# Group sums by shuffles on VectorE, a scaled expert added by DMA, and ScalarE's steps in another order

## The reference

```
h   = x + silu(bn(sum over e of sigmoid(mean(gn(x)) @ w_route.T + b_route)[e] * conv3x3(gn(x), w_experts[e])))
out = h + conv3x3(gn(h), sign(W))
```

## Time and profile before

| | |
|---|---|
| Time, median of 3 runs | 272.57 us (272.32 to 272.82) |
| Profiled execution: its own time | 272.72 us |
| Its span, first to last instruction | 270.6 us |
| Busy PE / DVE / ACT / POOL | 263.6 / 254.6 / 213.0 / 45.5 us |
| Granted TensorE clock | 1.000 in the mean |
| One stage (from `group_stats` to `group_stats`) | 15.50 us |

### The profile page before, as it was taken

One profiled execution on the slowest core, in us unless ns is written; L12 is line 12 of the kernel. 1 busy time (PEld: TensorE's weight loads), 2 busy tenths in 40 slices (PEclk: granted clock), 3 DMA queues, 4 the chain that ended last, 5 costly groups with the idle time before them and its releaser, 6 DMA issues.

```text
span 270.6 us, 4214 instructions
## 1 busy us (share of the span) xinstructions
PE 263.6 (97%) x1339; PEld 182.5 (67%) x1339; DVE 254.6 (94%) x461; ACT 213.0 (79%) x469; POOL 45.5 (17%) x61
## 2 busy tenths in 40 slices
PE   8899999999999999999999999999999999999993
PEld 7554857668595766759486776849576675948573
DVE  5799999999999999999999999999999999995984
ACT  2798898898979787997979798897979796736860
POOL 2012120313121120312112021212112021210120
PEclk9999999999999999999999999999999999999999
DMA  6998945552617355452726456261735536272407
GB/s 202 417 388 279 325 150 156 78 155 32 127 78 131 104 79 155 58 134 54 145 80 97 136 79 159 27 128 80 125 108 80 157 47 128 70 136 87 78 2 155
DMA packets 10245, 35.20 MB, mean 130 GB/s; under 512 B 1264, under 2 KB 1904, under 8 KB 10224
## 3 DMA queue, kind: packets, MB, share of 16 engines
q0 software_dynamic: 4176, 15.21, 33.1%
q1 hardware_dynamic: 5616, 19.34, 19.1%
q10 hardware_dynamic: 432, 0.39, 0.4%
HBM read 11.34 MB, written 16.25 MB: 102 GB/s over the span
## 4 chain that ended last, share of the span: by engine, by line
PE 95%; DVE 2%; issue 1%; POOL 0%; ACT 0%; DVEq 0%; POOLq 0%
PE pc L599 43%; PE pa L562 14%; PE pb L562 14%; PE pe_ L562 14%; PE pd L552 6%; PE pd L488 2%; PE ps L531 1%; PE ps L535 1%; DVE U L1178 0%; PE pa L636 0%; PE pb L636 0%; DVE X L1404 0%; PE pc L521 0%; POOL rstd L446 0%; DVE sums L1386 0%
## 5 line engine op out<-in xcount | busy, mean ns | idle before, releaser
L1188 DVE SCALAR_TENSOR_TENSOR U<-we,route,U 128x1152 f32<-128x1152 f32 x45 | 63.7, 1415 | 0.5
L599 PE MATMUL pc<-lo,ws 128*128 128x496 f16 (+3 forms) x270 | 62.0, 375 | 0.0
L599 PE MATMUL pc<-hi,ws 128*128 128x496 f16 (+3 forms) x270 | 59.8, 375 | 0.1
L599 PEld LDWEIGHTS pc<-hi,ws 128*128 128x128 f16 x270 | 26.4, 98 | 29.6 <-issue 0.5
L599 PEld LDWEIGHTS pc<-lo,ws 128*128 128x128 f16 x270 | 27.7, 106 | 26.3
L446 POOL TENSOR_TENSOR rstd<-ve,nhalf 128x2 f32<-128x2 f32 (+1 forms) x19 | 17.5, 923 | 141.4 <-ACT ve L856 120.1
L562 PE MATMUL pa<-V,UM 128*128 128x256 f32 (+1 forms) x180 | 40.7, 375 | 0.0
L562 PE MATMUL pb<-V,UM 128*128 128x256 f32 (+1 forms) x180 | 40.6, 375 | 0.0
L562 PE MATMUL pe_<-V,U 128*128 128x256 f32 (+1 forms) x180 | 40.5, 375 | 0.0
L562 PEld LDWEIGHTS pb<-V,UM 128*128 128x128 f32 x180 | 34.1, 190 | 5.5 <-issue 0.7
L562 PEld LDWEIGHTS pe_<-V,U 128*128 128x128 f32 x180 | 34.2, 190 | 3.9
(11 more groups left out here) (168 smaller groups left out, 400.9 us busy)
## 6 DMA issues: line engine op xcount, KB each, us to landing
X<-x SPq DMA_DIRECT2D x15, 512.0 KB, 5.6
out<-X SPq DMA_DIRECT2D x15, 512.0 KB, 2.6
out<-ev POOLq DMA_DIRECT2D x15, 512.0 KB, 5.5
X<-y POOLq DMA_DIRECT2D x14, 512.0 KB, 4.5
we<-w_experts SPq DMA_DIRECT2D x2, 768.0 KB, 8.2
ws_raw<-w_sign SPq DMA_DIRECT2D x1, 576.0 KB, 10.4
we<-w_experts SPq DMA_DIRECT2D x1, 512.0 KB, 6.2
out<-X SPq DMA_DIRECT2D x1, 384.0 KB, 3.0
```

Of the source, the lines that this page charges most:

```text
L599: mm = mm_(rows[:, r0 - first // W:r1 - first // W, c0:c1], ws[:, tap * C:(tap + 1) * C], plane((hi, lo)[part], i)[:, r0 + ky - 1:r1 + ky ...
L1188: v.scalar_tensor_tensor(out=nine(U[i % RING]), in0=expert(e), scalar=route[:, i, e:e + 1], in1=nine(U[i % RING]), op0=ALU.mult, op1=ALU.a ...
```

## The change

Three things.

1. The group values of slots 4 to 17 (stages 2 to 15; "slots 2 on" counts from the stage) no longer come from PE. DVE makes them: `group_sums(c)` exchanges neighbouring partitions by a shuffle and adds, then partitions two apart and adds, which leaves the sum over four channels in `gsum` in SBUF. In stages 2 to 14 it stands behind `inner_rows`, in stage 15 in front of `sign_points`. The readers on ACT take `gsum` and a scale of 1/4 in place of PSUM, and ACT gets one more instruction, `middle_mean`. Slots 1 to 3 and the last one stay on PE.
2. For images 3 to 15 DVE's `mix(i, 1)` is gone. ACT writes expert 1 times its route into a new tile `scaled` (`scale_second`, behind `mix`), and POOL issues a DMA that adds `scaled` (128x1152 float32) to `U`. DVE's `mix(i, 2)` waits for it.
3. In ACT's stage `bias` and `split_hi` stand ahead of `deviation`, `centring` and `pads`.

```diff
+SCALED_FROM = 3
...
+        def first_mix(i):
+            return 2 if i >= SCALED_FROM else 1
...
+        def by_shuffles(c):
+            return LAG < c < CHAINS - 1
+        def group_means(c, a, b):
+            return (gsum[:, c, a:b], 1.0 / GSIZE) if by_shuffles(c) else (gstats(c, a, b), 1.0)
...
# GpSimd
+            def add_scaled(i):
+                pool.wait_ge(mix_first, firsts_before(i) + 1)
+                pool.wait_ge(scaled_ready, i - SCALED_FROM + 1)
+                g.dma_start(flat(U[i % RING][:]), scaled[:], accum_op=ALU.add).then_inc(scaled_added, 16)
...
                 if ND <= t < B and t not in DVE_RESIDUAL:
                     residual(t)
+                if t + LAG - 1 < B:
+                    add_scaled(t + LAG - 1)
...
# TensorE
                     minus_points(t)
                     if t > 1:
-                        group_stats(c)
                         sign_half(t - 2, 1, 1, TAP_ORDER[-1:])
...
# ScalarE
             def variances(c):
                 a, b = cols(c)
-                act.wait_ge(gvar_ready, c + 1)
-                activation(gdev2[:, c, a:b], gstats(c, a, b), ACT.Square, bias=base[:, 0:1]).then_inc(gdev2_ready, 1)
+                wait_group(c)
+                means, share = group_means(c, a, b)
+                activation(gdev2[:, c, a:b], means, ACT.Square, bias=base[:, 0:1],
+                           scale=share).then_inc(gdev2_ready, 1)
...
+            def middle_mean(c):
+                activation(gmid[:, c:c + 1], gsum[:, c, MID:MID + 1], ACT.Copy, scale=1.0 / GSIZE) \
+                    .then_inc(gmid_ready, 1)
...
+            def scale_second(i):
+                wait(act, scaled_added, 16 * (i - SCALED_FROM))
+                activation(scaled[:].rearrange("p (g n) -> p g n", n=C), expert(1), ACT.Copy,
+                           scale=route[:, i, 1:2]).then_inc(scaled_ready, 1)
...
                 variances(c)
                 if t > 1:
+                    middle_mean(c)
+                if t > 1:
                     copy_minus(t)
                     evacuate(t - 2)
+                bias(c, MID)
+                split_hi(t - 1)
                 deviation(c)
                 if c < B:
                     centring(c)
                     pads(c)
-                bias(c, MID)
-                split_hi(t - 1)
-                if c < B:
                     pooled_plane(c)
                 split_hn(t - 1)
...
                     routing(c)
                     mix(c)
+                    scale_second(c)
...
# VectorE
+            def group_sums(c):
+                a, step = 0, 1 if c < B else 3
+                data = stats[:, c, 0:4:step]
+                if c < B:
+                    dve.wait_ge(nm_in_ready, c + 1)
+                dve.wait_ge(nm_mid_ready, c - LAG + 1)
+                dve.wait_ge(spread_ready, columns_to(c))
+                for n, bit in enumerate((1, 2)):
+                    source = (data, pairs[:, 0:4:step])[n]
+                    target = (pairs[:, 0:4:step], gsum[:, c, 0:4:step])[n]
+                    wait(dve, pairs_ready, c - LAG - 1 + n)
+                    v.stream_shuffle(swapped[:, n, 0:4:step], source, [p ^ bit for p in range(32)]) \
+                     .then_inc(swapped_ready, 1)
+                    dve.wait_ge(swapped_ready, 2 * (c - LAG - 1) + n + 1)
+                    op = v.tensor_tensor(target, source, swapped[:, n, 0:4:step], ALU.add)
+                    op.then_inc((pairs_ready, gsum_ready)[n], 1)
...
             def mix(i, e):
...
-                if e == 1:
+                if e < first_mix(i):
+                    return
+                if e > first_mix(i):
+                    dve.wait_ge(mixed, mixes_before(i) + e - first_mix(i))
+                elif e == 1:
                     dve.wait_ge(mix_first, firsts_before(i) + 1)
                 else:
-                    dve.wait_ge(mixed, mixes_before(i) + e - 1)
+                    dve.wait_ge(scaled_added, 16 * (i - SCALED_FROM + 1))
...
             for t in range(1, B):
                 if t == B - 1:
+                    group_sums(t + LAG - 1)
                     sign_points()
                 all_rows(t + 1)
...
                 inner_rows(t + 1)
+                if 1 < t < B - 1:
+                    group_sums(t + LAG - 1)
                 transform_minus(t + 1)
```

More of the change, by code:

```diff
@@ L157, in build @@
         centre = sb("centre", [C, B, 2])
+        scaled = sb("scaled", [C, K * KCO])
         pooled = sb("pooled", [C, B, E])
+        swapped = sb("swapped", [C, 2, 4])
+        pairs = sb("pairs", [C, 4])
+        gsum = sb("gsum", [C, CHAINS, 4])
+        gmid = sb("gmid", [C, CHAINS])
         th = sb("th", [C, B, E])
@@ L205, in build @@
         logits_ready = sem("logits_ready")
+        scaled_ready = sem("scaled_ready")
+        scaled_added = sem("scaled_added")
+        swapped_ready = sem("swapped_ready")
+        pairs_ready = sem("pairs_ready")
+        gsum_ready = sem("gsum_ready")
+        gmid_ready = sem("gmid_ready")
         th_ready = sem("th_ready")
@@ L282, in mixes_before @@
         def mixes_before(t):
-            return len(DIRECT_PARTS) * (E - 1) * min(t, ND) + (E - 1) * rank(t)
+            return len(DIRECT_PARTS) * (E - 1) * min(t, ND) + sum(E - first_mix(i) for i in range(ND, t))
+        def first_mix(i):
+            return 2 if i >= SCALED_FROM else 1
         def firsts_before(t):
@@ L523, in group_stats @@
             def group_stats(c):
-                if c < B:
-                    pe.wait_ge(nm_in_ready, c + 1)
+                pe.wait_ge(nm_in_ready, c + 1)
                 pe.wait_ge(nm_mid_ready, c - LAG + 1)
@@ L529, in group_stats @@
                 wait_bank(c)
-                step = 1 if c < B else 3
-                mm_(gstats(c, 0, 4, step), gmat[:], stats[:, c, 0:4:step], start=True, stop=True).then_inc(gvar_ready, 1)
+                mm_(gstats(c, 0, 4), gmat[:], stats[:, c, 0:4], start=True, stop=True).then_inc(gvar_ready, 1)
             def route_logits(i):
                 pe.wait_ge(pooled_ready, i + 1)
+                if i > LAG:
+                    pe.wait_ge(th_ready, i)
                 mm_(logits(i), ones[:], pooled[:, i, :], start=True, stop=True).then_inc(logits_ready, 1)
@@ L577, in plus_point @@
                 r = rank(t)
-                k = (P1, P2)[j]
                 pe.wait_ge(v_ready, 5 * r + 4)
                 wait(pe, sums_ready, 2 * r)
+                k = (P1, P2)[j]
                 pe.wait_ge(kernel_ready, 4 * r + k + 1)
@@ L829, in deviation @@
                     act.wait_ge(nm_in_ready, c + 1)
-                    activation(dev[:, c:c + 1], gnm(c, IN), ACT.Identity, bias=nm(c, IN), scale=-1.0) \
+                    mean, share = group_means(c, IN, IN + 1)
+                    activation(dev[:, c:c + 1], mean, ACT.Identity, bias=nm(c, IN), scale=-share) \
                         .then_inc(dev_ready, 1)
@@ L841, in variance, with wait_group @@
                 last = c == CHAINS - 1
-                act.wait_ge(gvar_ready, c + 1)
+                act.wait_ge(gvar_ready, LAG + 2 if last else c + 1)
                 activation(ve[:, c, k:k + 1], gvar(c, k), ACT.Identity, bias=epsilon[:, last:last + 1],
                            scale=1.0 / (HW * (LAST_SCALE if last else ACT_SCALE) ** 2)).then_inc(ve_ready, 1)
+            def wait_group(c):
+                if by_shuffles(c):
+                    act.wait_ge(gsum_ready, c - LAG)
+                else:
+                    act.wait_ge(gvar_ready, c + 1)
             def variances(c):
                 a, b = cols(c)
-                act.wait_ge(gvar_ready, c + 1)
-                activation(gdev2[:, c, a:b], gstats(c, a, b), ACT.Square, bias=base[:, 0:1]).then_inc(gdev2_ready, 1)
+                wait_group(c)
+                means, share = group_means(c, a, b)
+                activation(gdev2[:, c, a:b], means, ACT.Square, bias=base[:, 0:1],
+                           scale=share).then_inc(gdev2_ready, 1)
                 act.wait_ge(gdev2_ready, c - LAG + 1)
@@ L855, in variances @@
                 for k in range(a, b):
-                    op = activation(ve[:, c, k:k + 1], gvar(c, k), ACT.Identity, bias=less[:, c, k:k + 1],
-                                    scale=1.0 / (HW * ACT_SCALE ** 2))
+                    spreads, share = group_means(c, 3 - k, 4 - k)
+                    op = activation(ve[:, c, k:k + 1], spreads, ACT.Identity,
+                                    bias=less[:, c, k:k + 1], scale=share / (HW * ACT_SCALE ** 2))
                 op.then_inc(ve_ready, 1)
+            def middle_mean(c):
+                activation(gmid[:, c:c + 1], gsum[:, c, MID:MID + 1], ACT.Copy, scale=1.0 / GSIZE) \
+                    .then_inc(gmid_ready, 1)
             def bias(c, k):
                 act.wait_ge(rstd_ready, c + 1)
-                activation(nbias[:, c, k:k + 1], gnm(c, k), ACT.Copy,
+                if by_shuffles(c):
+                    act.wait_ge(gmid_ready, c - LAG)
```

(7 more changed lines are left out.)

## The result

The changed kernel takes 279.11 us (median of 5 runs, 278.73 to 279.36), the kernel before in the same series 272.72 us: a ratio of 1.0225, 95% interval 1.0207 to 1.0242. The forecast was 280.0 us, slower, with a range from 273.5 to 286 us.

The account below looks back on a forecast made before the run. ACT's ring through DVE's group sums was to bind at 16.12 us a stage against 15.50. Stage 2's delay and 11 turns of 0.62 gave +7.6 us, late stages saved 0.13 twice: +7.4, so 280.0 us, range 273.5 to 286.

Parts of the forecast that it names:

- ACT's ring: ACT's instructions from one group-value read to the next, through DVE's group sums; 16.12 us a stage, above PE's 15.37.
- ACT's stream before: ACT's unbroken work per stage in the kernel before, without the wait for silu's input; 13.6 us.
- seven readers of SBUF: Small ACT instructions that now read group values from SBUF instead of PSUM; together 0.27 us more per stage.
- step L: From ACT's last instruction before the group sums, through DVE's two shuffles and two adds, to the group values; 0.90 us.
- my surcharge: On DVE, each shuffle taken at 0.24 us against 0.19 for an add, for moving data across partitions.
- PE late at stage 2: PE's delay at taking up hi in stage 2, the first with shuffles; 0.94 us.
- first rival: PE stays the bound: only PE's loss of instructions counts, less some 0.5 us for stage 1; 271.2 us, chance 0.09.
- Eleven turns: Rounds of ACT's ring from stage 2 to stage 13, each 0.62 us longer than before; 6.82 us.
- costs at their upper ends: Case with step L at 1.5 us and the SBUF readers at 0.35: ring 16.8 us, kernel 288 us.
- Transfers in the way: Rival: POOL's third transfer delays the residual, so ACT's var_mid waits; 285 to 291 us, chance 0.08.
- PE stays the bound: Rival: the ring stays at or under PE's 15.37 us a stage; 271.2 us, chance 0.09.

Follow-up runs that it names:

- third experiment: The changed kernel with bias and split_hi put back behind deviation, centring and pads; 278.99 us. Also called third run.
- tenth run: The changed kernel with scale_second for image 3 alone, all transfers kept, centring and pads of images 4 to 15 on POOL, stage 1 in old order; 271.00 us.
- seventh run: The kernel before with only bias and split_hi moved ahead of deviation, centring and pads; 273.30 us.
- eighth run: The changed kernel with scale_second for image 3 alone; the 13 transfers stay and add that same tile for all images; 274.81 us.
- second experiment: The changed kernel with DVE making expert 1 of all images again, no scale_second, no added DMA; shuffles and new order stay; 278.44 us.

## Why the prediction was right, point by point

*The bound.* ACT's ring through the group values became the bound. Shown three ways: the chain of waits is on ACT; half of the shuffle pass is worth about 5 us; 0.6 to 0.7 us less in the ring brings PE's own stage back.

*The size of the ring.* Forecast 16.12 us, measured 15.97 (16.01 in the mean). The terms, each with the change it made:

| term | forecast | measured |
|---|---|---|
| ACT's stream before | 13.6 | 13.5 |
| `scale_second` | 1.16 | 1.14 |
| `middle_mean` | 0.19 | 0.09 |
| seven readers of SBUF | 0.27 | about 0.25 |
| step L | 0.90 | 1.03 |

The stream before was over-counted by about 0.1: I subtracted the wait in front of `silu`, but without a wait an instruction starts 0.1 us before its forerunner ends (`hn` 132.84 + 1.22, `silu` at 133.98). `middle_mean` costs the step from L901 to L981. The readers: L896's pair now takes 0.39 from start to start, and took 0.30; the others 0.02 to 0.06 each. In L, a shuffle costs as a small add does (steps 0.19 and 0.21 us), not 0.24. The Trainium skill, page "VectorE: DVE Perf Modes", section "The perf-mode tier table", puts both at the same plain rate; the trace agrees with it, against my surcharge. But the time from the end of L853 to the first shuffle is 0.24 us, where I had put 0.02.

*The sum.* PE late at stage 2: forecast 0.94, measured 52.11 - 51.16 = 0.95 us. This hit is in part luck. The forecast took PE's start in the kernel before from the chain (51.32), where the timeline has 51.16, and it had `hi` complete at 52.26, where it was at 52.05; the two slips cancel. Some 0.5 us of the delay is PE's wait for `UM` behind stage 1, which the forecast named as such only under its first rival, and 0.15 us was there in stage 1 already (35.71 against 35.56), where traces of versions that are alike up to that point differ by 0.3 us. Eleven turns: forecast 0.62 each, measured 0.50, 5.5 in place of 6.8. Together 6.5 us at stage 13, and 279.11 in place of 280.0. The gain that I had put to stages 14 and 15, 0.26 us, did not come: the two stages took 15.62 and 15.23 us, before 15.51 and 15.36. In stage 14 the load of `pb`'s weights still waits for `UM`, which costs 0.25 us; in the third experiment, where `UM` is in time, that stage takes 15.38 us.

*PE's wait.* Forecast: 0.7 us a stage, all of it in front of `hi`. Measured: the stage is 0.61 us over PE's own 15.37, but only 0.20 us is shown as a wait in front of `hi`; 0.25 us are lost at `pb`, where `UM` comes late (`pb` starts 7.73 us behind `hi` and lasts 2.61 us, in the tenth run 7.56 and 2.53). The forecast had called DVE's delay hidden. It is, as the ring sets the pace; at stage 14, where the ring no longer does, it was what took the gain.

*A slip in the range.* The prediction gives 288 us for the costs at their upper ends and calls it inside the range, which ends at 286. Nothing in the result turns on it.

*The move of `bias` and `split_hi`.* Alone on the kernel before it is not a gain, but +0.6 us in stage 1 (seventh run); with the ring binding it changes nothing (third run), which fits the 0.4 us that it was to give once against the 0.7 us that it costs in stage 1. Both as forecast in kind.

*DVE.* Forecast: it stalls in front of `low_part` by half a microsecond, and this is hidden. It stalled 0.9 us, and it was hidden, but only just: the second ring is at 15.56 us. The prediction said that DVE comes back before L823 does, and did not work out that a change that frees ACT would meet this ring next. That was the step that failed in the eighth run's expectation.

*The rivals.* Transfers in the way: a third of the transfer changed nothing, and in the tenth run all of them ran under PE's pace. PE stays the bound: true only once work leaves the ring; then 271.65 us against the 271.2 given for it. What the change could bring at most is what PE loses, 14 pairs.

*Why neither half would have done.* Shuffles without the scaled expert bind DVE (278.44), the scaled expert without the shuffles binds through PE (276.06), both bind ACT's ring (279.11).

## What to carry to other kernels

An engine with 20% idle time has no room if its idle time is the wait inside a ring: follow one value around until it meets itself, and add up the stream and the hand-overs. Taking an instruction off the bounding engine pays its duration, here 0.13 us a stage; putting its replacement on the ring between two others costs the whole latency of the hand-over each turn, here 1.03 us. Then look for the next ring under the first one: here it was at 15.56 us under 15.97.

## What the runs showed of the hardware

- A shuffle of 128x4 float32 takes 0.15 to 0.16 us, a small add 0.16, and the pattern load in front of the shuffle 0.014. Of the 1.03 us from ACT's last instruction to its first reader, the four steps take 0.79 us and the hand-over in front of them 0.24 us.
- Where DVE had waited for ACT in front of a pattern load, the load began 0.22 us after ACT's instruction had ended (126.83 to 127.05); in front of `low_part`, also a wait for ACT, it was 0.04 (134.06 to 134.10). Without a wait (second experiment) the load followed `inner_rows` at once. What the 0.2 us are was not tried; the shuffles wait for three semaphores, `low_part` for others.
- Small readers on ACT that moved from PSUM to SBUF became longer: `ve` from 0.26 to 0.29 us, `gdev` from 0.26 to 0.295.
- The accumulating DMA from SBUF to SBUF of 576 KB lands 4.8 us after its issue, beside 4.5 for 512 KB.
